# One attention and feed-forward block on one core: the early rounding, the rotated q and tile 6's normalisation put in another order

## The chip, the cores and the metric

The kernel runs on one core of a Trainium2 chip. The metric is the time of one execution on the device in microseconds (us). The profile is one execution taken by the hardware profiler; its span, from the first to the last recorded instruction, is a little shorter than the time of the execution.

## The reference

One block on x of 1024 tokens by 512: a layer norm with scale and shift from a modulation, attention, and a feed-forward part with a rank chosen for each token.

```python
h = _layernorm(x, axis=-1) * (1 + ca) + sa
x = x + ga * _L0_attn_ref(h, L0_attn_wq, L0_attn_wk, L0_attn_wv, L0_attn_wo)
h = _layernorm(x, axis=-1) * (1 + cb) + sb
x = x + gb * _L0_ffn_ref(h, ...)
# attention: 32 heads of 128, 8 heads of k and v
q = q * cos + _rotate_half(q) * sin
k = k * cos + _rotate_half(k) * sin
scores = jnp.einsum('bhtd,bhsd->bhts', q, k) * (1.0 / np.sqrt(HD))
att = jax.nn.softmax(jnp.where(mask, scores, -jnp.inf), axis=-1)
out = jnp.einsum('bhts,bhsd->bhtd', att, v)
return out.transpose(0, 2, 1, 3).reshape(B, T, H * HD) @ wo
```

## The kernel before

**Products in parts.** Every large product is made of rounded parts. An operand is split into `hi`, its rounding (ScalarE, an ACTIVATE with Copy), and `lo`, what is left (VectorE, a subtraction); TensorE forms hi·hi, hi·lo and lo·hi. So nearly every operand takes the way ScalarE, VectorE, TensorE.

**Loops.** Eight groups (one head of k and v each) of four heads (h = 0 to 3). The program is written out in full: `front(h, at)` and `back(h, at)` follow one another on each engine, and each engine has its own list of calls, written by hand. That order is all there is; engines meet through counting semaphores. An engine does its own list in order, so a wait holds up all that stands behind it.

**A head.** The 1024 queries are eight tiles of 128. Tile i has scores against 128·(i+1) keys. VectorE masks them and takes the maximum (`masked`), ScalarE takes the exponential and the row sums (`exp`), VectorE the reciprocal (`inverse`, L1218), GpSimd multiplies by it (`normalise`, L1588). Tiles 4 to 7 are then transposed by TensorE (L638), rounded (`transposed_hi`, L937) and their remainder taken (`transposed_lo`, L1225). Tiles 0 to 3, the early ones, are turned by VectorE in blocks and brought into columns by DMA through `p_rows`; SyncE issues that (L529, L535). The columns land in `pa_lo`; ScalarE rounds them into `pa_hi` (`early_hi`, L943), VectorE leaves the remainder in `pa_lo` (`early_lo`, L1244). The weighted sum over the early tiles is L675 with pa_hi and pa_lo, at the end of `back`.

**Projections inside.** `fill(h, place, at)` puts other products between, by the table `fillers`: in head 0 the output tiles (`project_out`, L705) of the group before, in heads 0 to 2 the next head's q, in the last head (h = 3) the next group's first things:

```python
(3, 4): [("q", (0, 0), 1)],
(3, 5): [("k", 0, 1), ("q", (0, 1), 1), ("v", 0, 1), ("v", 1, 1)],
```

They use two PSUM banks, `accumulators`, in turn: a job may start when the bank of the job two before is free (`a_taken`). k and q are rotated: ScalarE copies the halves of the bank crosswise into `qr` (`swap_halves`, L961 and L962), VectorE multiplies the bank by the cosine into `qc` (`times_cos`, L1266), which frees the bank; GpSimd multiplies `qr` by the sine (L1597) and adds the two (L1601); ScalarE rounds the sum (`rotated_hi`, L970) and VectorE takes its remainder (`rotated_lo`, L1275). An output tile's bank is freed by VectorE's addition into y (`add_output`, L1292). In group 0 the modulation's products stand in their place; a gate takes four operations of VectorE (L1321 to L1325). The value rows come by DMA too; VectorE takes their remainder at L1249. Weights are split by `split_hi` (L991) and `split_lo` (L1304).

**The place of the change** is `back` on ScalarE, VectorE and GpSimd. GpSimd's list there:

```python
normalise(h, 5, at)
if h == 2:
    scale_wo(2, at)
rotate(("q", ((h + 1) % R, 0)), at, int(last))
normalise(h, 6, at)
normalise(h, 7, at)
if last:
    rotate(("k", 0), at, 1)
    scale_wo(3, at)
```

Of the kernel before, what the change touches and what calls it, by code (L numbers as in the profile page):

```python
# [29 lines left out]
R = HEADS // KV_HEADS  # L30
# [247 lines left out]
def adaln_block(nc, x, wq, wk, wv, wo, ffn_w, ffn_b, ffn_a, ffn_bb, gate_w, gate_b, c, wmod, out):  # L278
    N = Numbers()
# [7 lines left out]
    with ExitStack() as ctx:  # L287
# [637 lines left out]
        def _(act):  # L925
# [6 lines left out]
            def transposed_hi(h, i, at, ahead=0):  # L932
                for part, js in enumerate(parts(i)):
                    name = (h, i, part)
                    need(act, t_full, N.value("t", name, at, ahead))
                    src = TB[:, N.slot("t", name, at, ahead), 0:len(js) * P].rearrange("p (a b) -> p a b", b=P)
                    nc.scalar.activation(pt_of(i, part, True), src, ACT.Copy).then_inc(t_hi, 1)  # L937

            def early_hi(h, at):

                n = head_number(h, at)
                act.wait_ge(columns_in, 64 * (n + 1))
                nc.scalar.activation(pa_blocks(pa_hi), f32(pa_blocks(pa_lo)), ACT.Copy).then_inc(pa_hi_done, 1)  # L943
# [20 lines left out]
            def rotated_hi(name, at, ahead=0):  # L964
                kind, which = name
                need(act, r_sum, N.value("r", name, at, ahead))
                if kind == "k" and which == 0:
                    need(act, s_full, N.value("s", (R - 1, 7), at, ahead - 1))
                dst, half = (q_hi, which[1]) if kind == "q" else (k_hi, which)
                nc.scalar.activation(dst[:, half * HALF:(half + 1) * HALF], qc[:, N.slot("r", name, at, ahead), :],  # L970
                                     ACT.Copy).then_inc(r_hi, 1)
# [21 lines left out]
            def fill(h, place, at, jobs=slice(None)):  # L993
                for what, which, ahead in fillers(h, place, at.first)[jobs]:
                    if what in "qk":
                        swap_halves((what, which), at, ahead)
# [23 lines left out]
            def back(h, at):  # L1020
                last = h == R - 1
                exp(h, 4, at)
                if last:
                    split_hi(("k", 0), at, 1)
                exp(h, 5, at)
                transposed_hi(h, 4, at)
                fill(h, 4, at)
                if h == 0:
                    value_hi(at)
                if h == 1:  # L1030
                    split_hi(("wo", 0), at)
                if h == 2:
                    split_hi(("wo", 1), at)
                exp(h, 6, at)
                transposed_hi(h, 5, at)
                rotated_hi(("q", ((h + 1) % R, 0)), at, int(last))
                if last:
                    split_hi(("v", 0), at, 1)
                if h:
                    early_hi(h, at)  # L1040
                if h == 2:
                    split_hi(("wo", 2), at)
                exp(h, 7, at)
                if not h:
                    early_hi(h, at)
                fill(h, 5, at, slice(0, -1))
                if last:
                    rotated_hi(("k", 0), at, 1)
                transposed_hi(h, 6, at)
                if last:  # L1050
                    split_hi(("wo", 3), at)
                fill(h, 5, at, slice(-1, None))
# [46 lines left out]
            for g in range(1, GROUPS):  # L1099
                at = Group(g)  # L1100
# [90 lines left out]
        def _(dve):  # L1191
# [188 lines left out]
            def back(h, at):  # L1380
                last = h == R - 1
                fill(h, 2, at)
                if h:
                    inverse(h, 4, at)
                masked(h, 5, at)
                if not h:
                    inverse(h, 4, at)
                if last:
                    split_lo(("k", 0), at, 1)
                fill(h, 3, at)  # L1390
                inverse(h, 5, at)
                fill(h, 4, at, slice(0, -1))
                transposed_lo(h, 4, at)
                masked(h, 6, at)
                fill(h, 4, at, slice(-1, None))
                if h == 0:
                    value_lo(at)
                if h == 1:
                    split_lo(("wo", 0), at)
                if h == 2:  # L1400
                    split_lo(("wo", 1), at)
                inverse(h, 6, at)
                masked(h, 7, at)
                transposed_lo(h, 5, at)
                rotated_lo(("q", ((h + 1) % R, 0)), at, int(last))
                if last:
                    split_lo(("v", 0), at, 1)
                if h:
                    early_lo(h, at)
                adds = fillers(h, 5, at.first)[:-1] if not h else []  # L1410
                fill(h, 5, at, slice(0, min(1, len(adds))))
                inverse(h, 7, at)
                if h == 2:
                    split_lo(("wo", 2), at)
                fill(h, 5, at, slice(min(1, len(adds)), -1))
                if not h:
                    early_lo(h, at)
                if last:
                    rotated_lo(("k", 0), at, 1)
                transposed_lo(h, 6, at)  # L1420
                if last:
                    split_lo(("wo", 3), at)
# [42 lines left out]
            for g in range(1, GROUPS):  # L1465
                at = Group(g)
# [118 lines left out]
        def _(pool):  # L1585
# [1 line left out]
                need_apart(pool, pool_passed, (s_inv, N.value("s", (h, i), at)))  # L1587
                nc.gpsimd.tensor_scalar(row(i), row(i), rowinv[:, i:i + 1], 1.0, ALU.mult, ALU.mult).then_inc(s_norm, 1)  # L1588

            def rotate(name, at, ahead=0):  # L1590

                kind, which = name
                half = which[1] if kind == "q" else which
                s = N.slot("r", name, at, ahead)
                n = N.value("r", name, at, ahead)
                need(pool, a_swapped, n)
                nc.gpsimd.tensor_tensor(qr[:, s, :], qr[:, s, :], trig[:, 1, half * HALF:(half + 1) * HALF],  # L1597
                                        ALU.mult).then_inc(r_sin, 1)
                need(pool, r_sin, n)
                need(pool, a_taken, N.value("a", name, at, ahead))  # L1600
                nc.gpsimd.tensor_tensor(qc[:, s, :], qc[:, s, :], qr[:, s, :], ALU.add).then_inc(r_sum, 1)  # L1601

            def scale_wo(r, at):

# [14 lines left out]
            def back(h, at):  # L1619
                last = h == R - 1  # L1620
                if h in (1, 2):
                    scale_wo(h - 1, at)
                normalise(h, 4, at)
                normalise(h, 5, at)
                if h == 2:
                    scale_wo(2, at)
                rotate(("q", ((h + 1) % R, 0)), at, int(last))
                normalise(h, 6, at)
                normalise(h, 7, at)
                if last:  # L1630
                    rotate(("k", 0), at, 1)
                    scale_wo(3, at)
# [93 lines left out]
```

## Time and profile before

| what | value |
|---|---|
| median of 3 runs | 1097.12 us (1095.56 to 1098.68) |
| time of the profiled execution | 1097.11 us |
| its span | 1095.3 us |
| TensorE busy (matmul) | 1053.4 us |
| VectorE busy | 773.5 us |
| ScalarE busy | 634.4 us |
| GpSimd busy | 520.0 us |
| granted TensorE clock, most slices | 0.9 of full speed or more |

The page of the profile gives these; the views behind it answer for each engine in order of time (timeline) and for who waited for whom (waits). A timeline row has the start in us from the span's start, the duration, the engine, the line, the operation, what is written and read, how many alike it merges, and in brackets the idle time before it with what ended that. PE is TensorE, ACT ScalarE, DVE VectorE, POOL GpSimd, SPq the queue of SyncE. Ends of matmuls are modelled: one reads longer than the distance to the next.

### The profile page before, as it was taken

What the parts mean: (1) busy time and instruction counts of PE and PEld (TensorE: products, weight loads), DVE (VectorE), ACT (ScalarE), POOL (GpSimd) and SP (SyncE); (2) the same over time, 40 slices, a digit from 0 to 9 for tenths busy, and PEclk for the clock granted to TensorE, in tenths of its full rate; (3) what the DMA queues carried; (4) which work ended last, traced back from release to release, by engine and by line L of the source; (5) the groups of instructions that cost most, each with busy time, mean ns of one, the idle gap of its engine ahead of it and who ended that gap; (6) DMA issues with size and microseconds to landing.
All of it is one profiled execution on the core that took longest, in us unless ns stands there. A gap on an engine that the chain in (4) does not pass through costs nothing.

```text
span 1095.3 us, 16543 instructions
## 1 busy us (share of the span) xinstructions
PE 1053.4 (96%) x5426; PEld 872.2 (80%) x5426; DVE 773.5 (71%) x1831; ACT 634.4 (58%) x1301; POOL 520.0 (47%) x506
## 2 busy tenths in 40 slices
PE   6999999999999999999999999999999999999997
PEld 3668878888888878887888878888787878888775
DVE  4668866688558866688657865689657875688576
ACT  5547764477437754477436754477436763577433
POOL 2535653365425653365434643455524652455244
PEclk8999999999999999999999999999999999999999
DMA  6462233132302233132312223023212224022001
GB/s 214 149 218 76 87 97 78 36 100 87 94 13 68 87 97 78 35 101 87 82 25 68 78 84 99 11 94 109 58 58 68 78 78 106 6 96 73 21 20 59
DMA packets 98285, 86.92 MB, mean 79 GB/s; under 512 B 39380, under 2 KB 84052, under 8 KB 98072
## 3 DMA queue, kind: packets, MB, share of 16 engines
q1 hardware_dynamic: 98200, 85.86, 26.4%
q8 instruction: 45, 0.74, 0.3%
q14 instruction: 40, 0.33, 0.1%
HBM read 59.23 MB, written 26.61 MB: 78 GB/s over the span
## 4 chain that ended last, share of the span: by engine, by line
PE 58%; DVE 12%; ACT 9%; DMA 8%; POOL 5%; issue 5%; SPq 2%; POOLq 0%; DVEq 0%; ACTq 0%
PE accumulators L705 16%; PE accumulators L675 14%; PE accumulators L690 11%; PE scores L625 9%; DMA pa_lo<-p_rows 4%; PE transposed L638 4%; DMA p_rows<-turned 3%; DVE p_large L1213 3%; ACT p_large L929 3%; DVE turned L1239 2%; PE scores L894 2%; DVE o_lo L1258 2%; POOL qc L1601 2%; DVE pb_lo L1225 1%; POOL qr L1597 1%
## 5 line engine op out<-in xcount | busy, mean ns | idle before, releaser
L1588 POOL TENSOR_SCALAR p_large<-p_large,rowinv 128x640 f32<-128x640 f32 (+3 forms) x128 | 125.3, 979 | 234.8 <-DVE rowinv L1218 234.8
L937 ACT ACTIVATE pb_hi<-transposed 128x512 fp32r<-128x512 f32 (+3 forms) x256 | 118.1, 509 | 178.6 <-PE transposed L638 178.4
L1597 POOL TENSOR_TENSOR qr<-qr,trig 128x512 f32<-128x512 f32 x80 | 106.2, 1327 | 206.8 <-ACT qr L962 206.8
L929 ACT ACTIVATE p_large<-p_large,negmax 128x640 f32<-128x640 f32 (+3 forms) x128 | 126.4, 988 | 99.3 <-DVE negmax L1213 98.2
L1225 DVE TENSOR_TENSOR pb_lo<-transposed,pb_hi 128x512 fp32r<-128x512 f32 (+3 forms) x256 | 141.8, 585 | 58.7 <-ACT pb_hi L937 58.3
L1213 DVE CUSTOM_DVE_ANT_0 p_large<-scores,mask 128x640 f32<-128x640 f32 (+3 forms) x128 | 130.0, 1016 | 18.4 <-PE scores L625 14.9
L625 PE MATMUL scores<-k_hi,q_hi 128*128 128x512 f32 (+2 forms) x384 | 139.5, 363 | 1.7 <-DVE negmax L1213 1.7
L625 PE MATMUL scores<-k_hi,q_lo 128*128 128x512 f32 (+2 forms) x384 | 131.7, 343 | 0.0
L1588 POOL TENSOR_SCALAR p_small<-p_small,rowinv 128x128 f32<-128x128 f32 (+3 forms) x128 | 97.2, 774 | 71.6 <-DVE rowinv L1218 71.6
L625 PE MATMUL scores<-k_lo,q_hi 128*128 128x512 f32 (+2 forms) x384 | 131.0, 341 | 0.0
L1601 POOL TENSOR_TENSOR qc<-qc,qr 128x512 f32<-128x512 f32 x80 | 116.6, 1458 | 6.5 <-POOL qr L1597 0.3
L638 PE MATMUL transposed<-ident,p_large 128*128 128x128 f32 x832 | 113.5, 274 | 4.0 <-POOL p_large L1588 1.6
L638 PEld LDWEIGHTS transposed<-ident,p_large 128*128 128x128 f32 x832 | 95.8, 140 | 23.9 <-POOL p_large L1588 14.9
L1292 DVE TENSOR_TENSOR y<-accumulators,y 128x512 f32<-128x512 f32 x64 | 44.2, 690 | 88.5 <-PE accumulators L705 88.5
L1266 DVE TENSOR_TENSOR qc<-accumulators,trig 128x512 f32<-128x512 f32 x80 | 55.1, 689 | 41.5 <-ACT qr L962 41.3
L625 PEld LDWEIGHTS scores<-k_hi,q_hi 128*128 128x128 f32 x384 | 72.4, 189 | 8.0 <-DVE negmax L1213 2.2
L625 PEld LDWEIGHTS scores<-k_hi,q_lo 128*128 128x128 f32 x384 | 72.2, 188 | 6.9
L625 PEld LDWEIGHTS scores<-k_lo,q_hi 128*128 128x128 f32 x384 | 72.9, 190 | 5.1
L929 ACT ACTIVATE p_small<-p_small,negmax 128x128 f32<-128x128 f32 (+3 forms) x128 | 70.9, 561 | 7.8 <-DVE negmax L1213 6.8
L705 PE MATMUL accumulators<-wo_hi,o_hi 128*128 128x512 f32 x256 | 71.2, 400 | 0.7 <-DVE h_lo L1478 0.4
L690 PE MATMUL accumulators<-h_hi,wq_hi 128*128 128x512 f32 x256 | 69.5, 393 | 0.0
L690 PE MATMUL accumulators<-h_hi,wq_lo 128*128 128x512 f32 x256 | 69.5, 394 | 0.0
(169 smaller groups left out, 2224.4 us busy)
## 6 DMA issues: line engine op xcount, KB each, us to landing
p_rows<-turned SPq DMA_DIRECT2D x31, 640.0 KB, 2.9
pa_lo<-p_rows SPq DMA_DIRECT2D x124, 160.0 KB, 3.2
stage<-in_L_attn_wq_dram SPq DMA_DIRECT2D x32, 256.0 KB, 2.8
stage<-in_L_attn_wo_dram SPq DMA_DIRECT2D x32, 256.0 KB, 3.4
v_rows<-vt SPq DMA_DIRECT2D x32, 128.0 KB, 2.8
v_lo<-v_rows SPq DMA_DIRECT2D x32, 128.0 KB, 3.2
y<-in_L_wmod_dram SPq DMA_DIRECT2D x4, 512.0 KB, 5.6
stage<-in_L_attn_wk_dram SPq DMA_DIRECT2D x8, 256.0 KB, 2.7
```

The source lines that it names most:

```text
L625: mm = nc.tensor.matmul(S_flat[:, c0 + key:c0 + key + n], a[:, i * P:(i + 1) * P], b[:, key:key + n], start=(k == 0), stop=(k == 2))
L638: mm = nc.tensor.transpose(TB[:, b, (j % 4) * P:(j % 4 + 1) * P], row(i)[:, j * P:(j + 1) * P], ident[:])
L675: mm = nc.tensor.matmul(acc[:, c0:HALF], v[:, j, :], pt, start=(hi and v is v_hi and j == 0), stop=(not hi and j == 4 * half + 3))
L690: mm = nc.tensor.matmul(acc, a[:, k, :], b[:, k, half * HALF:(half + 1) * HALF], start=(n == 0), stop=(n == 3 * KC - 1))
L705: mm = nc.tensor.matmul(acc, a[:, r, t * P:(t + 1) * P], b[:, r, :], start=(n == 0), stop=(n == 3 * R - 1))
L929: nc.scalar.activation(row(i), row(i), ACT.Exp, bias=negmax[:, i:i + 1], scale=-1.0, accum_out=rowsum[:, i:i + 1]).then_inc(s_exp, 1)
L937: nc.scalar.activation(pt_of(i, part, True), src, ACT.Copy).then_inc(t_hi, 1)
L1213: nc.vector.tensor_tensor_reduce(row(i), S_flat[:, c0:c0 + n], mask[:, T - n:T], -SCALE, 3.4e38, ALU.add, ALU.min, negmax[:, i:i + 1]).the ...
L1225: nc.vector.tensor_tensor(pt_of(i, part, False), src, f32(pt_of(i, part, True)), ALU.subtract).then_inc(t_lo, 1)
L1588: nc.gpsimd.tensor_scalar(row(i), row(i), rowinv[:, i:i + 1], 1.0, ALU.mult, ALU.mult).then_inc(s_norm, 1)
L1597: nc.gpsimd.tensor_tensor(qr[:, s, :], qr[:, s, :], trig[:, 1, half * HALF:(half + 1) * HALF], ALU.mult).then_inc(r_sin, 1)
L1601: nc.gpsimd.tensor_tensor(qc[:, s, :], qc[:, s, :], qr[:, s, :], ALU.add).then_inc(r_sum, 1)
```

## The change

- ScalarE, `back`: in heads 1 and 2 `early_hi` stands ahead of `rotated_hi` of the next q instead of behind it. In the last head it stands behind the exponential of tile 7 and k's `swap_halves`. In head 0 nothing moves.
- VectorE, `back`: in heads 1 and 2 `early_lo` stands ahead of `rotated_lo`. In the last head it stands behind the reciprocal of tile 7 and k's `times_cos`, ahead of q's.
- GpSimd, `back`: `rotate` is cut into `rotate_sin` and `rotate_sum`, and the normalisation of tile 6 stands between the two, in all heads that have this `back`.

No instruction is added or taken away, and no transfer. TensorE's list and SyncE's stay as they are.

```diff
--- before.py
+++ after.py
@@ -1033,17 +1033,19 @@
                     split_hi(("wo", 1), at)
                 exp(h, 6, at)
                 transposed_hi(h, 5, at)
+                if h in (1, 2):
+                    early_hi(h, at)
                 rotated_hi(("q", ((h + 1) % R, 0)), at, int(last))
                 if last:
                     split_hi(("v", 0), at, 1)
-                if h:
-                    early_hi(h, at)
                 if h == 2:
                     split_hi(("wo", 2), at)
                 exp(h, 7, at)
-                if not h:
+                fill(h, 5, at, slice(0, 1) if last else slice(0, -1))
+                if h in (0, 3):
                     early_hi(h, at)
-                fill(h, 5, at, slice(0, -1))
+                if last:
+                    fill(h, 5, at, slice(1, -1))
                 if last:
                     rotated_hi(("k", 0), at, 1)
                 transposed_hi(h, 6, at)
@@ -1402,17 +1404,20 @@
                 inverse(h, 6, at)
                 masked(h, 7, at)
                 transposed_lo(h, 5, at)
+                if h in (1, 2):
+                    early_lo(h, at)
                 rotated_lo(("q", ((h + 1) % R, 0)), at, int(last))
                 if last:
                     split_lo(("v", 0), at, 1)
-                if h:
-                    early_lo(h, at)
                 adds = fillers(h, 5, at.first)[:-1] if not h else []
                 fill(h, 5, at, slice(0, min(1, len(adds))))
                 inverse(h, 7, at)
                 if h == 2:
                     split_lo(("wo", 2), at)
-                fill(h, 5, at, slice(min(1, len(adds)), -1))
+                if last:
+                    fill(h, 5, at, slice(0, 1))
+                    early_lo(h, at)
+                fill(h, 5, at, slice(1 if last else min(1, len(adds)), -1))
                 if not h:
                     early_lo(h, at)
                 if last:
@@ -1587,7 +1592,7 @@
                 need_apart(pool, pool_passed, (s_inv, N.value("s", (h, i), at)))
                 nc.gpsimd.tensor_scalar(row(i), row(i), rowinv[:, i:i + 1], 1.0, ALU.mult, ALU.mult).then_inc(s_norm, 1)
 
-            def rotate(name, at, ahead=0):
+            def rotate_sin(name, at, ahead=0):
 
                 kind, which = name
                 half = which[1] if kind == "q" else which
@@ -1596,9 +1601,17 @@
                 need(pool, a_swapped, n)
                 nc.gpsimd.tensor_tensor(qr[:, s, :], qr[:, s, :], trig[:, 1, half * HALF:(half + 1) * HALF],
                                         ALU.mult).then_inc(r_sin, 1)
+
+            def rotate_sum(name, at, ahead=0):
+                s = N.slot("r", name, at, ahead)
+                n = N.value("r", name, at, ahead)
                 need(pool, r_sin, n)
                 need(pool, a_taken, N.value("a", name, at, ahead))
                 nc.gpsimd.tensor_tensor(qc[:, s, :], qc[:, s, :], qr[:, s, :], ALU.add).then_inc(r_sum, 1)
+
+            def rotate(name, at, ahead=0):
+                rotate_sin(name, at, ahead)
+                rotate_sum(name, at, ahead)
 
             def scale_wo(r, at):
 
@@ -1624,8 +1637,9 @@
                 normalise(h, 5, at)
                 if h == 2:
                     scale_wo(2, at)
-                rotate(("q", ((h + 1) % R, 0)), at, int(last))
+                rotate_sin(("q", ((h + 1) % R, 0)), at, int(last))
                 normalise(h, 6, at)
+                rotate_sum(("q", ((h + 1) % R, 0)), at, int(last))
                 normalise(h, 7, at)
                 if last:
                     rotate(("k", 0), at, 1)
```

ScalarE in the last head of group 0 (pb_hi: rounding of transposed tiles; q_hi: the rotated q; wv_hi: v's weights; pa_hi: the early rounding; p_large 128x1024: exponential of tile 7; qr: crosswise copies), before:

```order
L937 ACTIVATE pb_hi<-transposed 128x2x128
L970 ACTIVATE q_hi<-qc 128x512
L991 ACTIVATE wv_hi<-stage 128x512
L943 ACTIVATE pa_hi<-pa_lo 128x4x320
L929 ACTIVATE p_large,rowsum<-p_large,negmax 128x1024
L961 ACTIVATE qr<-accumulators 64x512
L962 ACTIVATE qr<-accumulators 64x512
L961 ACTIVATE qr<-accumulators 64x512
```

and with the change:

```order
L937 ACTIVATE pb_hi<-transposed 128x2x128
L970 ACTIVATE q_hi<-qc 128x512
L991 ACTIVATE wv_hi<-stage 128x512
L929 ACTIVATE p_large,rowsum<-p_large,negmax 128x1024
L961 ACTIVATE qr<-accumulators 64x512
L962 ACTIVATE qr<-accumulators 64x512
L943 ACTIVATE pa_hi<-pa_lo 128x4x320
L961 ACTIVATE qr<-accumulators 64x512
```

The early rounding has moved from ahead of the exponential to behind k's two copies; q's follow it.

GpSimd in the same head (640 to 1024: normalisation of tiles 4 to 7; qr: sine product; qc: the rotation's sum), before:

```order
L1588 TENSOR_SCALAR p_large<-p_large,rowinv 128x640
L1588 TENSOR_SCALAR p_large<-p_large,rowinv 128x768
L1597 TENSOR_TENSOR qr<-qr,trig 128x512
L1601 TENSOR_TENSOR qc<-qc,qr 128x512
L1588 TENSOR_SCALAR p_large<-p_large,rowinv 128x896
L1588 TENSOR_SCALAR p_large<-p_large,rowinv 128x1024
```

and with the change:

```order
L1593 TENSOR_SCALAR p_large<-p_large,rowinv 128x640
L1593 TENSOR_SCALAR p_large<-p_large,rowinv 128x768
L1602 TENSOR_TENSOR qr<-qr,trig 128x512
L1593 TENSOR_SCALAR p_large<-p_large,rowinv 128x896
L1610 TENSOR_TENSOR qc<-qc,qr 128x512
L1593 TENSOR_SCALAR p_large<-p_large,rowinv 128x1024
```

Tile 6's normalisation has moved between the sine product and the sum. This is so in every head.

ScalarE in the third head of group 0 (wo_hi: a part of the output weights), before:

```order
L937 ACTIVATE pb_hi<-transposed 128x2x128
L970 ACTIVATE q_hi<-qc 128x512
L943 ACTIVATE pa_hi<-pa_lo 128x4x320
L991 ACTIVATE wo_hi<-stage 128x512
L929 ACTIVATE p_large,rowsum<-p_large,negmax 128x1024
```

and with the change:

```order
L937 ACTIVATE pb_hi<-transposed 128x2x128
L943 ACTIVATE pa_hi<-pa_lo 128x4x320
L970 ACTIVATE q_hi<-qc 128x512
L991 ACTIVATE wo_hi<-stage 128x512
L929 ACTIVATE p_large,rowsum<-p_large,negmax 128x1024
```

The early rounding and q's have changed places; the second head has the same exchange.

## Rows read from the trace of the kernel before

**Rows 1.** the page, busy time of each engine, share of the span, instructions.

```profile
PE 1053.4 (96%) x5426; PEld 872.2 (80%) x5426; DVE 773.5 (71%) x1831; ACT 634.4 (58%) x1301; POOL 520.0 (47%) x506
```

**Rows 2.** waits of TensorE: us in total, times, longest us.

```profile
PE accumulators L690 <- DVE qc L1266: 10.8, 8, 2.2
...
PE accumulators L675 <- ACT pa_hi L943: 4.0, 6, 1.6
```

**Rows 3.** timeline, ScalarE, last head of group 2: start us, us, operation [idle before].

```profile
389.19 0.63 ACT L970 ACTIVATE q_hi<-qc 128x512 fp32r<-128x512 f32 x1
389.73 0.62 ACT L991 ACTIVATE wv_hi<-stage 128x512 fp32r<-128x512 f32 x1
390.97 1.27 ACT L943 ACTIVATE pa_hi<-pa_lo 128x1280 fp32r<-128x1280 f32 x1 [0.62 <-DMA pa_lo<-p_rows]
392.15 1.14 ACT L929 ACTIVATE p_large<-p_large,negmax 128x1024 f32<-128x1024 f32 x1
...
393.40 0.59 ACT L961 ACTIVATE qr<-accumulators 64x512 f32<-64x512 f32 x1
```

**Rows 4.** the same stretch, VectorE: tile 6's reciprocal, k's cosine product.

```profile
388.32 0.16 DVE L1218 RECIPROCAL rowinv<-rowsum 128x1 f32<-128x1 f32 x1 [0.60 <-ACT p_large L929]
...
394.62 0.69 DVE L1266 TENSOR_TENSOR qc<-accumulators,trig 128x512 f32<-128x512 f32 x1 [0.78 <-ACT qr L962]
```

**Rows 5.** the same stretch, TensorE: v's first half.

```profile
395.37 1.20 PE L690 MATMUL accumulators<-h_hi,wv_hi 128*128 128x512 f32 x4 [1.77 <-DVE qc L1266]
```

**Rows 6.** the same stretch, GpSimd: rotation's sum, tile 6's normalisation.

```profile
387.87 1.29 POOL L1601 TENSOR_TENSOR qc<-qc,qr 128x512 f32<-128x512 f32 x1
389.14 1.02 POOL L1588 TENSOR_SCALAR p_large<-p_large,rowinv 128x896 f32<-128x896 f32 x1
```

**Rows 7.** timeline, VectorE, third head: reciprocals of tiles 6 and 7.

```profile
366.29 0.15 DVE L1218 RECIPROCAL rowinv<-rowsum 128x1 f32<-128x1 f32 x1
...
371.04 0.16 DVE L1218 RECIPROCAL rowinv<-rowsum 128x1 f32<-128x1 f32 x1 [0.16 <-ACT p_large L929]
```

**Rows 8.** timeline, GpSimd, second and third head: tile 7's normalisation.

```profile
348.60 1.13 POOL L1588 TENSOR_SCALAR p_large<-p_large,rowinv 128x1024 f32<-128x1024 f32 x1 [3.04 <-DVE rowinv L1218]
...
371.40 1.38 POOL L1588 TENSOR_SCALAR p_large<-p_large,rowinv 128x1024 f32<-128x1024 f32 x1 [2.89 <-DVE rowinv L1218]
```

**Rows 9.** timeline, VectorE, first head of group 2.

```profile
310.02 1.26 DVE L1249 TENSOR_TENSOR v_lo<-v_lo,v_hi 128x1024 fp32r<-128x1024 f32 x1
311.20 0.15 DVE L1218 RECIPROCAL rowinv<-rowsum 128x1 f32<-128x1 f32 x1
...
313.34 0.68 DVE L1275 TENSOR_TENSOR q_lo<-qc,q_hi 128x512 fp32r<-128x512 f32 x1
313.94 0.68 DVE L1292 TENSOR_TENSOR y<-accumulators,y 128x512 f32<-128x512 f32 x1
```

**Rows 10.** the same stretch, ScalarE: q's rounding.

```profile
312.47 0.64 ACT L970 ACTIVATE q_hi<-qc 128x512 fp32r<-128x512 f32 x1 [0.79 <-POOL qc L1601]
```

**Rows 11.** the same stretch, TensorE: output tile 6.

```profile
315.51 1.07 PE L705 MATMUL accumulators<-wo_hi,o_hi 128*128 128x512 f32 x4
```

**Rows 12.** the same stretch, GpSimd: rotation's sum.

```profile
310.28 2.15 POOL L1601 TENSOR_TENSOR qc<-qc,qr 128x512 f32<-128x512 f32 x1
```

**Rows 13.** timeline, VectorE, first head of group 0: a gate's last operation.

```profile
74.41 0.69 DVE L1325 SCALAR_TENSOR_TENSOR ga_b<-ga_b,accumulators 128x512 f32<-128x512 f32 x1
```

**Rows 14.** the same stretch, TensorE: q's projection.

```profile
75.15 1.19 PE L690 MATMUL accumulators<-h_hi,wq_hi 128*128 128x512 f32 x4
```

**Rows 15.** timeline, ScalarE, third head: early rounding, tile 7's exponential.

```profile
368.10 1.26 ACT L943 ACTIVATE pa_hi<-pa_lo 128x1280 fp32r<-128x1280 f32 x1
...
369.78 1.14 ACT L929 ACTIVATE p_large<-p_large,negmax 128x1024 f32<-128x1024 f32 x1
```

**Rows 16.** timeline, TensorE, second and third head: tile 7's transposes.

```profile
350.36 1.03 PE L638 MATMUL transposed<-ident,p_large 128*128 128x128 f32 x8
...
372.92 1.04 PE L638 MATMUL transposed<-ident,p_large 128*128 128x128 f32 x8
```

## The prediction

> **What bounds the kernel now.** I read the page first: TensorE is busy for 96% of the span [rows 1], so the time is TensorE's work, which the change leaves as it is, plus its waits. The waits of TensorE come next [rows 2]. The largest that the change can touch is the first half of v in the last head of a group, which needs k's bank: 10.8 us in 8 waits, seven of them in the seven last heads with a next group, the eighth in the opening. The second is the weighted sum that waits for the early rounding (pa_hi): 4.0 us in 6. Then I followed three places through the timelines of ScalarE, VectorE, GpSimd and TensorE, all in group 2; other groups repeat them within some hundredths, but for DMA landings.
>
> In the last head, ScalarE rounds the rotated q (389.19) and v's weights (389.73), waits 0.62 us for the early columns, rounds them (390.97), exponentiates tile 7 (392.15) and only then turns k (393.40) [rows 3]. VectorE frees the bank with the cosine product at 394.62 [rows 4], and TensorE goes on at 395.37, after 1.77 us idle [rows 5].
>
> **The change part by part.** Its two halves pull against each other, so I work out first what GpSimd's new order does.
>
> *The rotation's sum.* Before, GpSimd ran the sine product, the sum (387.87) and tile 6's normalisation (389.14) without a gap [rows 6]. Tile 6's reciprocal came at 388.32 [rows 4], in the middle of the sum: the sum filled the time in which the normalisation could not have run. Now the normalisation stands first and the sum is behind its wait. From a reciprocal's start to its normalisation's is 0.36 us (371.04 to 371.40, [rows 7, 8]); the normalisation holds GpSimd 1.00 us and the sum takes 1.29; ScalarE's rounding of q follows 0.03 us later [rows 3, 6]. So that rounding starts 0.36 + 1.00 + 1.29 + 0.03 = 2.68 us after the reciprocal of tile 6, in every head. I price each head from this.
>
> *Last head (seven times).* The q rounding starts at 388.32 + 2.68 = 391.00, not 389.19, v's weights at 391.54, and tile 7's exponential, which no longer has the early rounding ahead of it, at 392.08. That is 0.07 us before the old one. k is turned 1.25 us later (393.33), the cosine product 1.22 later (394.55), v goes on 0.75 later, at 395.30 [rows 3, 4, 5]: idle 1.70 where it was 1.77. What taking the rounding away won, the later sum gives back. Where the columns landed late before, this is a small gain; where they did not, a loss. The new wait hangs on no DMA, so it is the same seven times: 11.9 us. The old ones were 10.8 less the eighth, which is small. I take **+1.3 us**. Without GpSimd's half the exponential would start at 390.27 and this wait would all but vanish; that is a rival below.
>
> *The second half of v* needs q's bank. Its cosine product stands now behind the early remainder (pa_lo) on VectorE, whose rounding starts when k's turn has ended, 394.55, and takes 1.27 [rows 3]. The remainder is ready at 395.8 but reads and writes what GpSimd's rotation of k also uses; both end near 397.5, and by my count q's bank comes 0.1 us late, between 0 and 0.3. **+0.6 us** for seven.
>
> *At no cost, as long as its cover holds:* in the last head the early rounding starts at 394.55 instead of 390.97 [rows 3]. Its reader, the first weighted sum, comes behind both halves of v, which start at 395.37 [rows 5] and take over 5 us; with less than 2 us of work there the wait would come back as one for pa_hi. SyncE issues the same transfers in the same order, and none of them waits for a moved step earlier than before.
>
> *First head, groups 1 to 7.* Here there is a wait that did not exist. The reciprocal is at 311.20 [rows 9], so q's rounding starts at 313.88 instead of 312.47 [rows 10]: 1.41 us late. VectorE's remainder of q (313.34) stands in front of the addition of output tile 4 (313.94), which frees the bank that output tile 6 wants at 315.51 [rows 9, 11]. The remainder began 0.87 us after the rounding did. Of this 0.64 is the rounding itself, and the rest falls on tile 6's normalisation, which ran on GpSimd until 312.43 + 1.02 = 313.45 [rows 6, 12]. In the new order that is over by then, so I take 0.65 and keep 0.87 as the other end. Remainder at 314.53, addition 0.60 later at 315.13, bank free 0.75 later (the distance of [rows 4, 5]) at 315.88: TensorE waits 0.37 us. A stalled start costs a little more: four matmuls read 1.20 us after a wait and 1.07 without one [rows 5, 11]. 7 x 0.50 = **+3.5 us** (5.0 with 0.87). The sum itself meets no VectorE operation on SBUF there, so it takes 1.29.
>
> *First head, group 0.* There the same remainder stands ahead of the gate's four operations, and TensorE already starts q's projection as the last of them frees the bank: 74.41 to 75.15, which is 0.74 [rows 13, 14]. The delay goes straight through: 1.4 less 0.2 as above, **+1.2 us**.
>
> *Third head (eight times).* The early rounding, now first, starts when its columns land, at 368.10 or up to 0.7 us earlier [rows 15]. Tile 6's transposes lose a wait of 0.2 us. But q's rounding starts at 366.29 + 2.68 = 368.97 [rows 7] and tile 7's exponential 1.08 us later (two roundings of 0.54, as [rows 3]), at 370.05 instead of 369.78 [rows 15]: +0.27. Its normalisation ends at 372.78 and its transposes start at 372.92 [rows 8, 16], so 0.09 us of that is slack (0.05 is the handover). What TensorE wins before, it waits for here. +0.18 each; if the columns land as late as 368.10, q is rounded at 369.3 and it is +0.47. I take 0.25, nearer the low end, as most landed before ScalarE asked: **+2.0 us**.
>
> *Second head (eight times).* The early rounding waits for its columns already, so moving it to the front gives nothing. It pushes tile 7's exponential back by q's 0.54, and its reciprocal by the remainder's 0.60. Tile 7's normalisation ends at 349.73 and its transposes start at 350.36 [rows 8, 16]: a slack of 0.63 holds it but for some hundredths. **+0.1 us**; +1 at worst. The 4.0 us of waits for pa_hi stay, for they are DMA.
>
> Sum: 1.3 + 0.6 + 3.5 + 1.2 + 2.0 + 0.1 = 8.7 us. The profiled execution took 1097.11 us, which is the median of the three runs within 0.01; so 1105.8 us.
>
> **A rule against the trace.** The sum of the first head's rotation took 2.15 us where the last head's took 1.29: VectorE's remainder of v ran over its first 1.00 us [rows 6, 9, 12]. It did not share, it waited 0.86 us. The Trainium skill (SBUF — State Buffer, section "SBUF: two separate sides") says why: the two engines lock one port pair, whoever starts first holds it for a whole instruction, and an operation of VectorE with two inputs in SBUF takes part. By that rule, the trace agrees. It speaks against this change, because the early remainder, a long operation of that kind, now falls near the sum.
>
> **The rivals.**
> *The remainder takes the port first (8%).* If in the third head the columns land by about 366.3, VectorE would begin pa_lo at 367.6, about when GpSimd wants to begin the sum (367.63), and hold it some 1.2 us. That delays tile 7's exponential and transposes: 8 x 1.2 = 9.6 on top, 1115 us. Against it: nothing shows a landing so early, and a sum that has begun makes pa_lo wait.
> *The first head's slack holds (13%).* If the addition's bank comes early enough, by 0.5 us against my count, the 3.5 goes and 1102 is left. For it: three links of one row each.
> *The sum's lateness does not reach the exponential (12%): faster.* This needs tile 6's reciprocal to come before the sine product is done, 387.8, instead of 388.32, or to find slack that I do not see. It decides at a q rounding before 389.9 in the last head; then k's wait ends by 394.2 and earlier. With the whole lateness gone, 10.4 of the waits go, about 1087 us. For it: the masking and the exponential that feed the reciprocal could shift. Against it: they follow TensorE's scores of tile 6, which do not move.
> *The change does not free the bank earlier* is, in effect, my forecast for the last head; were it the only effect, the time would be within 2 us of before (4%). The remaining 3% is a mixture on the slower side.
>
> **How the numbers follow.** The forecast has 60%, from 1102 to 1111: its ends take the first head at 2.0 and 5.5, the third at 1.4 and 3.8, and a little either way for landings. A difference under 0.3%, 3.3 us, can't be told from none. Slower by more: 60 + 8 + 3, and 9 of the 13 of the slack rival: 80%. Within: 4 + 4 = 8%. Faster: 12%. The range is 1099.5 to 1112: it takes in the slack rival and leaves out the port rival and the faster one.
>
> **What would show it.** Right: the q rounding (line 970 before) 2.7 us behind tile 6's reciprocal everywhere and GpSimd idle between sine product and normalisation; seven waits for k's bank of about equal length, 1.6 to 1.8; a new wait of output tile 6 for the addition in the first head; tile 7's transposes in the third head waiting for GpSimd. Wrong: waits for k's bank near zero, no idle time before the output tiles, or a sum over 2 us in the third head.

## The result, and the profile after

| | before | changed |
|---|---|---|
| median of 9 runs each | 1096.70 us | 1104.92 us |
| lowest to highest | 1095.56 to 1102.03 | 1100.96 to 1106.12 |
| ratio, 95% interval | | 1.0064 (1.0044 to 1.0083) |
| span of the profiled execution | 1095.3 us | 1099.8 us |

The change makes the kernel 0.64% slower, 7.0 us on 1096.7 (4.8 to 9.1); the forecast was 8.7 us, 1105.8. The interval of the ratio begins at 0.44%, so the slowdown is small but clear of the noise.

TensorE's waits in the changed kernel, from the view of who waited for whom (us in total, times, longest us; lines are those of the changed file, up to 14 higher):

```profile
PE accumulators L690 <- DVE qc L1268: 11.7, 7, 1.7
...
PE accumulators L675 <- ACT pa_hi L943: 3.4, 5, 1.4
...
PE transposed L638 <- POOL p_large L1593: 2.8, 8, 0.5
```

The wait for k's bank was 10.8 us in 8 with a longest of 2.2 [rows 2]; it is 11.7 in 7, the longest 1.7. The early rounding's was 4.0 in 6 and is 3.4 in 5. That of tile 7's transposes is new in this form. Next comes the last head of group 2, ScalarE, in the timeline (start us, us, engine, line, operation, idle before):

```profile
394.02 0.63 ACT L970 ACTIVATE q_hi<-qc 128x512 fp32r<-128x512 f32 x1 [1.96 <-POOL qc L1610]
394.56 0.62 ACT L991 ACTIVATE wv_hi<-stage 128x512 fp32r<-128x512 f32 x1
395.09 1.13 ACT L929 ACTIVATE p_large<-p_large,negmax 128x1024 f32<-128x1024 f32 x1
...
396.33 0.59 ACT L961 ACTIVATE qr<-accumulators 64x512 f32<-64x512 f32 x1
...
397.55 1.27 ACT L943 ACTIVATE pa_hi<-pa_lo 128x1280 fp32r<-128x1280 f32 x1
```

Against [rows 3], the early rounding is gone from ahead of the exponential, and in its place stands 1.96 us of idle time ahead of q's rounding. The same stretch on GpSimd:

```profile
389.53 1.30 POOL L1602 TENSOR_TENSOR qr<-qr,trig 128x512 f32<-128x512 f32 x1 [0.66 <-ACT qr L962]
391.72 1.01 POOL L1593 TENSOR_SCALAR p_large<-p_large,rowinv 128x896 f32<-128x896 f32 x1 [0.89 <-DVE rowinv L1220]
392.70 1.30 POOL L1610 TENSOR_TENSOR qc<-qc,qr 128x512 f32<-128x512 f32 x1
```

After the sine product (to 390.83) GpSimd is idle for 0.89 us until tile 6's reciprocal is there; in [rows 6] the sum filled that. VectorE there:

```profile
391.35 0.17 DVE L1220 RECIPROCAL rowinv<-rowsum 128x1 f32<-128x1 f32 x1 [0.60 <-ACT p_large L929]
...
397.56 0.69 DVE L1268 TENSOR_TENSOR qc<-accumulators,trig 128x512 f32<-128x512 f32 x1 [1.06 <-ACT qr L962]
...
400.35 0.68 DVE L1268 TENSOR_TENSOR qc<-accumulators,trig 128x512 f32<-128x512 f32 x1
```

and TensorE there:

```profile
398.31 1.19 PE L690 MATMUL accumulators<-h_hi,wv_hi 128*128 128x512 f32 x4 [1.66 <-DVE qc L1268]
...
401.16 1.13 PE L690 MATMUL accumulators<-h_hi,wv_hi 128*128 128x512 f32 x4
```

From the reciprocal (391.35) to q's rounding (394.02) it is 2.67 us, where the prediction said 2.68. The cosine product at 397.56 frees k's bank and v starts 0.75 us later after 1.66 us idle; [rows 5] had 1.77. The second half of v follows 2.85 us behind, with no wait.

The first head of group 2, VectorE's timeline:

```profile
313.68 0.15 DVE L1220 RECIPROCAL rowinv<-rowsum 128x1 f32<-128x1 f32 x1
...
317.01 0.69 DVE L1277 TENSOR_TENSOR q_lo<-qc,q_hi 128x512 fp32r<-128x512 f32 x1 [1.12 <-ACT q_hi L970]
317.62 0.68 DVE L1294 TENSOR_TENSOR y<-accumulators,y 128x512 f32<-128x512 f32 x1
```

and TensorE's:

```profile
315.27 1.07 PE L705 MATMUL accumulators<-wo_hi,o_hi 128*128 128x512 f32 x4
...
318.36 1.19 PE L705 MATMUL accumulators<-wo_hi,o_hi 128*128 128x512 f32 x4 [0.21 <-DVE y L1294]
```

q's rounding is at 316.35, 2.67 us behind the reciprocal of 313.68; q's remainder starts 0.66 us later, the addition 0.61 after that, and output tile 6 another 0.74 later. Its predecessor began at 315.27 and takes 2.72 us, the distance of two such products, so tile 6 is 0.37 us late, as predicted; the row shows 0.21, since the end of a matmul is modelled, and its four matmuls read 1.19 against 1.07 in [rows 11]. Before, tile 6 went on without a wait. Six other groups show the same (0.20 to 0.21, once 0.50).

The third head of group 2, ScalarE's timeline:

```profile
370.50 1.28 ACT L943 ACTIVATE pa_hi<-pa_lo 128x1280 fp32r<-128x1280 f32 x1 [1.18 <-DMA pa_lo<-p_rows]
371.78 0.63 ACT L970 ACTIVATE q_hi<-qc 128x512 fp32r<-128x512 f32 x1
...
372.83 1.14 ACT L929 ACTIVATE p_large<-p_large,negmax 128x1024 f32<-128x1024 f32 x1
```

and TensorE's, at tile 7's transposes:

```profile
375.89 1.09 PE L638 MATMUL transposed<-ident,p_large 128*128 128x128 f32 x8 [0.37 <-POOL p_large L1593]
```

The early rounding comes first now and waits for its columns; the exponential of tile 7 starts 2.33 us behind it, and its transposes wait 0.37 for GpSimd, where they did not [rows 16].

**The span says less than the runs.** The profiled spans differ by 4.5 us, the medians by 8.2. Part of it is TensorE's granted clock, in the profile before (windows: stretch, length, busy us of each engine with count, then granted clock, DMA share, GB/s):

```profile
645.00:650.00 5.00, 5.00 (x16) 4.00 (x17) 1.22 (x2) 0.91 (x2) 4.84 (x5) 0.67 0.00 0
1017.00:1022.00 5.00, 5.00 (x19) 4.06 (x20) 1.45 (x3) 1.55 (x4) 0.00 (x0) 0.67 0.10 38
```

and in the changed one, at the same places of the program:

```profile
648.00:653.00 5.00, 4.25 (x18) 3.41 (x19) 3.85 (x5) 3.09 (x4) 4.92 (x4) 1.00 0.15 45
1023.00:1028.00 5.00, 5.00 (x28) 4.25 (x29) 2.73 (x6) 2.98 (x6) 1.04 (x1) 1.00 0.09 33
```

A clock of 0.67 over 5 us is 3.3 us at half of the full rate, the lower of the two levels. Between the opening and the end, the profile before has three such stretches, near 62, 645 and 1017; the changed one has none. Each costs up to 1.7 us, so that up to 5 us of the difference are hidden in the span. The profiled execution of the change is also one of the shortest of its nine: 1101.56 us at a mean clock of 0.996, where the median one took 1104.92 at 0.992. The profiled execution before had 0.991, so it is not the clock that makes the change slower.

### The profile page after: what moved, and what is told of

The parts are those of the page before. It is cut to its first block, busy times and chain, and to the rows that moved or that the text cites. A ratio compares the mean times of both kernels' runs of the same rounds, so it can differ in the third digit from the quotient of the medians.

```text
span 1099.8 us, 16543 instructions
## 1 busy us (share of the span) xinstructions
PE 1054.7 (96%) x5426; PEld 867.8 (79%) x5426; DVE 775.0 (70%) x1831; ACT 633.5 (58%) x1301; POOL 516.2 (47%) x506
## 4 chain that ended last, share of the span: by engine, by line
PE 42%; DVE 19%; ACT 14%; DMA 9%; issue 8%; POOL 5%; SPq 2%; POOLq 0%; DVEq 0%; ACTq 0%
PE accumulators L705 13%; PE accumulators L690 10%; PE accumulators L675 8%; DMA pa_lo<-p_rows 4%; ACT p_large L929 4%; PE scores L625 4%; DMA p_rows<-turned 4%; DVE pb_lo L1227 3%; ACT pb_hi L937 3%; DVE p_large L1215 3%; DVE turned L1241 3%; PE transposed L638 3%; POOL qc L1610 2%; DVE p_small L1215 2%; DVE o_lo L1260 2%
## 5 line engine op out<-in xcount | busy, mean ns | idle before, releaser
L1215 DVE CUSTOM_DVE_ANT_0 p_large<-scores,mask 128x640 f32<-128x640 f32 (+3 forms) x128 | 130.0, 1016 | 14.8 <-PE scores L625 10.8
L1610 POOL TENSOR_TENSOR qc<-qc,qr 128x512 f32<-128x512 f32 x80 | 112.0, 1400 | 3.8
```

Of the source, the lines that this page charges most:

```text
L1215: nc.vector.tensor_tensor_reduce(row(i), S_flat[:, c0:c0 + n], mask[:, T - n:T], -SCALE, 3.4e38, ALU.add, ALU.min, negmax[:, i:i + 1]).the ...
```

## The experiments

The theory: GpSimd's split puts the rotation's sum behind the wait for tile 6's reciprocal, in every head. It takes back what the last head's new order gains, and makes a new wait in the first head. The rivals: the waits are bound by something else, or the exchange of roundings in heads 1 and 2 costs the time. All ratios are against the kernel before, run beside them on the same chip. Their intervals are 0.13% to 0.34% to either side, so two experiments whose ratios differ by less than about 0.4% are told apart by their waits and not by their times.

**The change without the split** (e1):

```diff
-                rotate_sin(("q", ((h + 1) % R, 0)), at, int(last))
+                rotate(("q", ((h + 1) % R, 0)), at, int(last))
                 normalise(h, 6, at)
-                rotate_sum(("q", ((h + 1) % R, 0)), at, int(last))
```

> The change with GpSimd's list as before (rotation whole, then tile 6's normalisation). Split theory: the late rotation sum is what gave the last head's gain back, so the exponential of tile 7 starts about 1.1 us after q's rounding began at its old place, the seven waits of v for k's bank fall from 1.66 each to 0.3 or less, the first head's new wait for the addition (0.21 each) goes, and the time is about 10 us under the kernel before: 1087. Rival (the bank was never bound by the early rounding; the k projection or the masking of tile 7 binds it): waits stay above 1 us and the time stays within 3 us of the kernel before.

Measured: 0.9916 (0.9882 to 0.9949), median 1089.53. The last head of group 2 again, ScalarE's timeline:

```profile
392.15 0.64 ACT L970 ACTIVATE q_hi<-qc 128x512 fp32r<-128x512 f32 x1 [0.17 <-POOL qc L1610]
...
393.20 1.14 ACT L929 ACTIVATE p_large<-p_large,negmax 128x1024 f32<-128x1024 f32 x1
...
394.46 0.59 ACT L961 ACTIVATE qr<-accumulators 64x512 f32<-64x512 f32 x1
...
395.68 1.28 ACT L943 ACTIVATE pa_hi<-pa_lo 128x1280 fp32r<-128x1280 f32 x1
```

and TensorE's:

```profile
395.46 1.07 PE L690 MATMUL accumulators<-h_hi,wq_lo 128*128 128x512 f32 x4
396.43 1.20 PE L690 MATMUL accumulators<-h_hi,wv_hi 128*128 128x512 f32 x4
```

The exponential starts 1.05 us after q's rounding, and v 0.97 us behind the row ahead of it, where 0.91 is the pace: no wait is shown. In its waits the group for k's bank is not among the five longest; a single one of 0.33 is left, in group 6. The theory stands and the rival (a wait of 1 us or more stays) falls. GpSimd's split turned a gain of 0.84% into a loss of 0.64%.

**The split alone on the kernel before** (e2): the `rotate_sin`, `normalise`, `rotate_sum` of the change, ScalarE and VectorE as before.

> The kernel before with GpSimd's split alone. Split theory: every head's q rounding starts 2.68 us after tile 6's reciprocal; in the last head the early rounding and then the exponential queue behind it, so the wait for k's bank grows to about 2.9 us, seven times (+9); first head +4.7 as in the change; in the third head the early rounding and with it the weighted sum and tile 7 come 1.4 us late (+11). Together about 1122, clearly slower than the change itself. Rival (the split costs little by itself, the exchange of roundings in the second and third head is what costs): within 5 us of the kernel before.

Measured: 1.0333 (1.0299 to 1.0367), median 1136.20. That is 36.6 us over the kernel before beside it, where the terms of the expectation make 24.7: 12 us more. Its waits, in the view of who waited for whom:

```profile
PE accumulators L675 <- ACT pa_hi L943: 23.2, 16, 1.6
...
PE accumulators L690 <- DVE qc L1266: 19.9, 7, 2.9
...
PE accumulators L705 <- DVE y L1292: 1.8, 7, 0.5
```

The wait for k's bank is 19.9 us in 7, 2.85 each, as expected to a few hundredths; the first head's is there too. The expectation had left out two things. In the second head also the early rounding stands behind q's, and there the weighted sum now waits 1.25 to 1.42 us in every group, some 10 us in all. And the clock fell more often (windows, columns as above):

```profile
283.00:288.00 5.00, 3.79 (x10) 2.98 (x11) 1.38 (x2) 2.25 (x4) 4.92 (x5) 0.69 0.01 2
801.00:806.00 5.00, 4.04 (x18) 3.31 (x19) 2.33 (x4) 2.00 (x4) 4.92 (x5) 1.00 0.00 0
928.00:933.00 5.00, 3.10 (x8) 2.43 (x9) 1.75 (x4) 2.92 (x5) 4.35 (x4) 0.71 0.15 43
```

The seven waits of 2.8 us end at 156, 284, 414, 543, 673, 802 and 930; behind five of them the clock is at half for 3.4 us (0.66 over the 5 us from 414 on; the windows shown cut a part of it off), behind those at 156 and 802 it is not. The split by itself is the costly part, and the exchange of roundings shields it: with the change, the early rounding no longer queues behind the late q.

**The split in the second and third head only** (e3):

```diff
+                if h in (1, 2):
+                    normalise(h, 6, at)
                 rotate_sum(("q", ((h + 1) % R, 0)), at, int(last))
+                if not (h in (1, 2)):
+                    normalise(h, 6, at)
```

> The change with the split in the second and third head only. Split theory: the first head's waits (0.21) and the last head's (1.66) both go, the third head's wait for tile 7's normalisation (0.25 to 0.46) stays: about 1089, 1 to 2 us above the change without any split. Rival (third head is where the split costs most): more than 4 us above it.

Measured: 0.9922 (0.9894 to 0.9951), median 1091.29, against 0.9916 without any split: no difference that can be told. The third head of group 2 without a split (e1) shows why, on GpSimd and ScalarE:

```profile
368.75 1.62 POOL L1610 TENSOR_TENSOR qc<-qc,qr 128x512 f32<-128x512 f32 x1
...
370.51 1.28 ACT L943 ACTIVATE pa_hi<-pa_lo 128x1280 fp32r<-128x1280 f32 x1 [1.16 <-DMA pa_lo<-p_rows]
371.69 0.62 ACT L970 ACTIVATE q_hi<-qc 128x512 fp32r<-128x512 f32 x1
```

The sum ends at 370.37, but q is rounded 1.32 us later, since the early rounding, now ahead of it, waits for its columns. In all eight third heads of e1 q's rounding starts 2.5 us or more behind tile 6's reciprocal, nearly as late as with the split, so a late sum finds little to delay. Tile 6's and tile 7's transposes both wait about 0.2 us there; with the split tile 6's no longer wait and tile 7's wait longer. The group of waits without a split (e1):

```profile
PE transposed L638 <- POOL p_large L1593: 3.7, 16, 0.3
```

and with it in those two heads (e3):

```profile
PE transposed L638 <- POOL p_large L1593: 2.9, 8, 0.5
```

**Split in the first head only** (e5) and **in the last head only** (e6), the same edit with `h == 0` and with `last`:

> The change with GpSimd's split in head 0 only. Split theory: only the first head's wait of output tile 6 for the addition (0.21 shown, 0.5 in time, seven times) and group 0's 0.8 to 1.2 come on top of the version without a split, no wait for k's bank: 4 to 5 us above that version, 1094. Rival (the first head's wait is made good by TensorE later): no difference from the version without a split.

> The change with the split in the last head only. Split theory: seven waits of 1.66 to 1.70 for k's bank return, none in the first head: 7 x 1.8 = 12 us above the version without a split, close to 1101, and the same waits to a hundredth as in the change. Rival (the waits need the lateness of the other heads too): under 1 us each.

Measured: e5 0.9952 (0.9933 to 0.9972), e6 1.0002 (0.9983 to 1.0022). Over the version without a split that is 0.36% or 3.9 us for the first head, and 0.86% or 9.4 us for the last; expected were 4 to 5 and 12. Each of the two differences has an interval of about 4 us to either side, so the last head's cost is shown by the times, and the first head's rests on its waits and on the next experiment. The waits tell the two apart. The first head's split (e5):

```profile
PE accumulators L705 <- DVE y L1294: 1.8, 7, 0.5
```

the last head's (e6):

```profile
PE accumulators L690 <- DVE qc L1268: 11.6, 7, 1.7
```

Each split makes its own wait and not the other's.

**The addition ahead of q's remainder in the first head** (e4), the change else as it is:

```diff
+                adds = fillers(h, 5, at.first)[:-1] if not h else []
+                fill(h, 5, at, slice(0, min(1, len(adds))))
                 rotated_lo(("q", ((h + 1) % R, 0)), at, int(last))
                 if last:
                     split_lo(("v", 0), at, 1)
-                adds = fillers(h, 5, at.first)[:-1] if not h else []
-                fill(h, 5, at, slice(0, min(1, len(adds))))
```

> The change, with VectorE's first addition of an output tile in head 0 ahead of q's remainder (group 0: the gate ahead of it). My step: the first head's wait is q's late remainder in front of the addition that frees the bank. Then the wait of output tile 6 (0.21 shown, 0.5 us in time) goes seven times and group 0's 0.76: 4 to 5 us under the change, about 1100. Rival (TensorE's output tile is late for another reason, such as the rounded weights): no difference from the change.

Measured: 1.0013 (0.9991 to 1.0034), median 1100.68, 0.51% or 5.6 us under the change (about 3 us to either side). The waits for the addition are gone, those for k's bank as before (11.8 in 7). So the way of the first head's delay, q's remainder in front of the addition that frees the bank, is shown twice: by putting its cause alone on top of the version without it (e5 against e1, in the waits), and by going round it (e4, in waits and time).

**The last head's part alone** (e7), heads 1 and 2 and GpSimd as before, and **the exchange in heads 1 and 2 alone** (e8):

```diff
-                if h:
-                    early_hi(h, at)
+                if h in (1, 2):
+                    early_hi(h, at)
...
                 exp(h, 7, at)
-                if not h:
-                    early_hi(h, at)
-                fill(h, 5, at, slice(0, -1))
+                fill(h, 5, at, slice(0, 1) if last else slice(0, -1))
+                if h in (0, 3):
+                    early_hi(h, at)
+                if last:
+                    fill(h, 5, at, slice(1, -1))
```

and VectorE's list in the same way; e8 has the complement.

> The kernel before with the last head's part alone: the early rounding and its remainder behind tile 7's exponential and k's copies; heads 1 and 2 and GpSimd as before. Split theory: all the gain is here, the waits for k's bank go, 10 us under the kernel before (1089), level with the version that also exchanges the roundings in heads 1 and 2. Rival (the exchange has a part in the gain): 2 us or more above that version.

> The kernel before with the exchange in heads 1 and 2 alone. By my working the second head's early rounding waits for its columns anyway and the third head's gain is waited away at tile 7: within 2 us of the kernel before, either side. Rival (early columns were the bound in the third head): 3 us faster or more.

Measured: e7 **0.9896 (0.9877 to 0.9916)**, median 1088.38, the lowest ratio of all and faster than both kernels, though its interval overlaps those of e1, e3, e9 and e10; e8 1.0016 (1.0002 to 1.0029). So all the gain that shows is in the last head. The exchange alone costs about 0.16% or 1.8 us, from 0.02% to 0.29%, hardly clear of zero; on top of the last head's part (e1 against e7) it is 0.20%, within the noise. The waits of e8 agree with such a cost:

```profile
ACT pa_hi L943 <- DMA pa_lo<-p_rows: 26.7, 21, 2.5
...
PE accumulators L690 <- DVE qc L1268: 10.6, 7, 2.4
...
PE accumulators L675 <- ACT pa_hi L943: 3.9, 7, 1.3
...
PE transposed L638 <- POOL p_large L1592: 3.4, 15, 0.3
```

and those of the kernel before:

```profile
ACT pa_hi L943 <- DMA pa_lo<-p_rows: 6.8, 9, 1.7
...
PE transposed L638 <- POOL p_large L1588: 1.6, 8, 0.2
```

ScalarE waits 26.7 us in 21 for the early columns, 6.8 in 9 before: with the rounding in front, it now stands idle for a transfer with q's rounding and the exponential queued behind. The weighted sum gains nothing (3.9 us, [rows 2] has 4.0), and TensorE waits 1.8 us more at the transposes, tile 7's now beside tile 6's. Between e7 and e1 the same group grows from 1.7 in 8 to 3.7 in 16.

**Two tries for better**: the third output weight rounded behind tile 7's exponential, without a split (e9) and with the split in heads 1 and 2 (e10).

```diff
+                exp(h, 7, at)
                 if h == 2:
                     split_hi(("wo", 2), at)
-                exp(h, 7, at)
```

> The change without any split, and ScalarE's rounding of the third output weight behind the exponential of tile 7 in head 2. If the third head's tile 7 transposes wait for that chain (0.19 to 0.27 shown eight times), the exponential comes 0.5 us earlier and they stop waiting: 1 to 3 us under the version without a split. Rival (another link, the DMA columns or q, sets them): no difference.

> The split in heads 1 and 2 only, with the same late rounding of the third output weight. There tile 6's transposes do not wait; tile 7's wait 0.26 to 0.48 eight times. With the exponential 0.5 us earlier this wait goes too: 2 to 4 us under the version with the split in the middle heads, the best of all, about 1085. Rival: the late sum holds the exponential anyway, gain under 1 us.

Measured: 0.9920 (0.9895 to 0.9945) and 0.9909 (0.9885 to 0.9933), against 0.9916 and 0.9922 without it: neither can be told from its base, and e10 is not the best of all that it was expected to be. The transposes' wait in e9 is 2.9 us in 14 for 3.7 in 16, but the early rounding's grew from 3.2 to 5.1; in e10 tile 7's transposes still wait, 2.2 us in 8 for 2.9. A gain of some tenths of a us eight times is under what these runs resolve; I leave it open.

**The change once more** (e11), unedited:

> The change once more, beside its parts on one chip. By the parts measured so far (last head's order, plus GpSimd's split in the first and the last head, +0.36% and +0.86%): 0.4% to 0.6% above the kernel before. Seven waits for k's bank of 1.66 to 1.70 and seven of 0.2 for the addition.

Measured: 1.0055 (1.0033 to 1.0076). Its profiled span is 1107.9, 8 us over the first profile of the same program:

```profile
PE accumulators L690 <- DVE qc L1268: 11.7, 7, 1.7
...
PE accumulators L675 <- ACT pa_hi L943: 7.5, 9, 1.5
```

The wait for k's bank repeats to 0.1 us, 11.7 in 7; the early rounding's is 7.5 where it was 3.4. The other half of the 8 us is the clock, in two stretches that the first profile of the change does not have (windows of this run):

```profile
50.00:55.00 5.00, 5.00 (x11) 0.96 (x10) 4.00 (x15) 2.37 (x6) 2.49 (x4) 0.66 0.56 126
63.00:68.00 5.00, 5.00 (x18) 3.98 (x18) 1.01 (x6) 0.21 (x1) 0.00 (x0) 0.66 1.01 364
```

So what hangs on engines repeats, while what hangs on the columns' transfer moves by 4 us between two profiles of one program, and the clock by up to 3.4.

## Why the prediction was right

- *q's rounding 2.68 us behind the reciprocal, everywhere*: 2.67 in both places shown, and 2.63 to 2.69 in all but two of the first, third and last heads; the first head of group 4 has 2.95, which is the one with the longer wait of 0.50. This is the step on which the rest stands. In the second head it did not hold: there the early rounding stands in front and waits for its columns, and q's rounding starts 3.0 to 4.6 us behind. TensorE's waits for the early rounding are no longer than before (3.4 us for 4.0), so the sum of the prediction does not suffer.
- *Last head, seven equal waits of 1.70, +1.3 us*: 1.66 to 1.70, 11.7 us in all against 10.4 (10.8 less the opening's 0.39), which is +1.3. (The prediction's own 11.9 would have made it 1.5.) That the new order gives back all it won is shown by e1 and e6, 0.86% or 9.4 us apart.
- *The second half of v, +0.6*: wrong, it is 0. The early remainder held q's cosine product until 400.35, and the bank would have been ready 0.75 later, 401.10; TensorE came at 401.16. The term was mis-sized by the one tenth on which it turned.
- *First head, +3.5 and +1.2*: a delay of 0.37, plus 0.12 by which the first four matmuls behind the wait read longer, seven times, is 3.4; in group 0 the wait is 0.76 where there was none shown. e5 gives 3.9 us and e4 5.6, each with several us of interval; 4.7 lies between. The choice of 0.65 over 0.87 for q's remainder was right: 0.66.
- *Third head +2.0, second +0.1*: tile 7's transposes wait 0.25 to 0.46 eight times, 2.8 us in all, where tile 6's waited 0.2 eight times before, 1.6 in all: +1.2 by the waits. By the ratios second and third head come to 0.16% (e8) + 0.06% (e3 over e1), 2.4 us, with more noise than that. The third head's place and sign were right, but the late sum is only half of the reason: without the split its q is rounded nearly as late, behind the early rounding that waits for its columns (e1), and tile 7's transposes wait already. The prediction had landings that late as its other end, +0.47. The second and the third head were not measured apart.
- *The rivals.* The port rival did not come: the sum in the third head takes 1.28 to 1.30 us in its place between the reciprocal and q. The slack rival did not come either: TensorE waits for the addition in all seven groups. The faster rival needed the sum in time for the exponential; e1 comes nearest to what it describes, at 1089.5 (beside 1099.6 for the kernel before) against the 1087 that it was given.
- *The total*: 8.7 us forecast, 7.0 (4.8 to 9.1) measured. Of the missing 1.7 the v term is 0.6; the rest is within the interval.

The expectation of e2 was too low by 12 us, for the second head and the clock; the prediction did not rest on either.

## What to carry to other kernels

Before an operation is put in front of another on the same engine, look up when its input arrives: here the normalisation's reciprocal came 0.5 us into the sum, and the new order bought 0.2 us for tile 6 and sold 1.4 to 1.8 us of the sum. An order on one engine that looks like a gain there can cost more on another engine, several steps later, so time each part of a combined change alone: of the three here one gains 1.0%, the exchange loses about 0.2% and GpSimd's split 1.5% on top of the two. A step that waits for a transfer belongs behind the work that needs none.

## What the runs showed of the hardware

TensorE's granted clock fell to its lower level, 1.2 GHz, for 3.4 us behind five of seven waits of 2.8 us (e2). In the profile before it fell behind the wait of 1.94 us that ended at 644.84, but not behind that of 2.23 in the group ahead; none of the seven waits of 1.65 to 1.70 that the last head's split makes was followed by one, in four profiles that have them (the change twice, e4, e6). With two profiles of one program 8 us apart, a profiled span alone is no measure of a change of this size.

The lock between VectorE and GpSimd showed in one more place. In the changed kernel's last head, GpSimd's sum for k:

```profile
399.16 2.42 POOL L1610 TENSOR_TENSOR qc<-qc,qr 128x512 f32<-128x512 f32 x1
```

It takes 2.42 us instead of 1.29, with VectorE's early remainder (398.86, 1.57 us) over its start. The view of who waited for whom has no wait of TensorE for k there, so no cost shows. The Trainium skill (SBUF — State Buffer, section "SBUF: two separate sides") has this as a lock of the whole port pair by whoever starts first; the row agrees. The remainder takes 1.56 to 1.58 us in all seven such last heads, where the end of GpSimd's sine product (to 399.09) lies over its start, and 1.49 in the third heads, where nothing of GpSimd runs beside it: it seems to wait in its turn.
